# Scan: one 512 KB load of the cumulated rows for each chunk, x and y moved two tiles at a time every second chunk

## The reference, cut to what matters

```
x = silu(causal_conv(xn @ Wx.T))
b, c, dt = x @ Wb.T, x @ Wc.T, softplus(x @ Wdt.T + b_dt)    # 8 heads, state 64
state = exp(dt_t * a) * state + (dt_t * b_t) x_t             # 8192 steps, one after the other
y_t = c_t . state
out = groupnorm(y + d * x) * silu(z) @ Wout.T
```

## Time and profile before

| | us |
|---|---|
| median of 3 runs | 1229.94 |
| lowest and highest | 1228.64, 1230.48 |
| profiled execution, its own time | 1230.54 |
| its span in the profile | 1228.7 |
| scan, by the transposes L1553 | about 190 to 779 |

### The profile page before, as it was taken

One profiled execution on the slowest core, in us unless ns is written; L12 is line 12 of the kernel. 1 busy time (PEld: TensorE's weight loads), 2 busy tenths in 40 slices (PEclk: granted clock), 3 DMA queues, 4 the chain that ended last, 5 costly groups with the idle time before them and its releaser, 6 DMA issues.

```text
span 1228.7 us, 31470 instructions
## 1 busy us (share of the span) xinstructions
PE 1208.2 (98%) x12207; PEld 1012.2 (82%) x12207; DVE 949.7 (77%) x2028; ACT 611.8 (50%) x1279; POOL 796.4 (65%) x790
## 2 busy tenths in 40 slices
PE   8999999999999999999999999999999999999998
PEld 4666678888888888888888788898999889899998
DVE  7999977889876777777778667987777765776676
ACT  6999984434444443354344335543333332555454
POOL 4889955555555676776776648476666655576664
PEclk9999999999999999999999999999999999999999
DMA  9799756554455445555455456565544446799994
GB/s 298 261 337 356 288 214 170 149 157 146 157 157 160 154 146 170 161 150 164 149 148 168 126 171 212 190 156 91 109 91 90 97 87 125 251 320 322 336 332 166
DMA packets 140404, 231.40 MB, mean 188 GB/s; under 512 B 24416, under 2 KB 83040, under 8 KB 135648
## 3 DMA queue, kind: packets, MB, share of 16 engines
q1 hardware_dynamic: 127104, 212.10, 52.6%
q0 software_dynamic: 12288, 17.05, 8.1%
q10 hardware_dynamic: 864, 0.24, 0.1%
HBM read 147.81 MB, written 81.53 MB: 187 GB/s over the span
## 4 chain that ended last, share of the span: by engine, by line
PE 85%; DVE 5%; ACT 3%; DMA 3%; issue 2%; SPq 1%; POOL 1%; ACTq 0%; POOLq 0%; DVEq 0%
PE ps L1446 27%; PE ps L1808 11%; PE ps L2067 9%; PE ps L2301 7%; PE ps L2280 7%; PE ps L1527 4%; PE ps L1494 3%; PE ps L1553 3%; PE ps L1516 3%; PE ps L1538 2%; PE ps L1567 2%; PE ps L695 1%; DMA x_dram<-x 1%; PE ps L1787 1%; ACT tap L503 1%
## 5 line engine op out<-in xcount | busy, mean ns | idle before, releaser
L1408 ACT ACTIVATE decay<-tap,ncum 128x128 f32<-128x128 f32 x344 | 105.5, 389 | 191.7 <-POOL tap L1315 191.7
L1993 POOL DMA_INDIRECT ffn_dram<-ob,idx x64 | 110.5, 1727 | 81.8 <-DVE ob L1912 67.8
L2029 ACT ACTIVATE mid<-ps,b_up 128x512 f32<-128x512 f32 x96 | 66.1, 689 | 152.9 <-PE ps L1808 149.6
L1322 POOL TENSOR_TENSOR x_lo<-x,x_hi 128x512 fp32r<-128x512 f32 x56 | 76.9, 1372 | 100.4 <-ACT x_hi L1392 98.6
L1179 DVE TENSOR_TENSOR x_dt<-ps,dt 128x512 f32<-128x512 f32 x64 | 44.2, 691 | 126.4 <-PE ps L1553 126.3
L1446 PE MATMUL ps<-x_hi,w_hi_b 128*128 128x512 f32 x240 | 100.0, 416 | 2.0 <-issue 1.9
L1446 PE MATMUL ps<-x_hi,w_hi_c 128*128 128x512 f32 x240 | 99.3, 414 | 0.0
L2156 POOL TENSOR_SCALAR yc<-yc,gn_scale,gn_shift 128x512 f32<-128x512 f32 x56 | 76.3, 1374 | 33.1 <-DMA yc<-y_dram 33.1
L1446 PE MATMUL ps<-x_lo,w_hi_b 128*128 128x512 f32 x240 | 95.1, 396 | 0.0
L1408 ACT ACTIVATE decay<-cum_row,ncum 128x128 f32<-128x128 f32 x168 | 51.5, 391 | 86.8 <-POOL cum_row L1315 86.8
L1446 PE MATMUL ps<-x_lo,w_hi_c 128*128 128x512 f32 x240 | 94.2, 392 | 0.0
(11 more groups left out here) (321 smaller groups left out, 3996.9 us busy)
## 6 DMA issues: line engine op xcount, KB each, us to landing
tap<-cum_dram SPq DMA_DIRECT2D x86, 256.0 KB, 3.6
x_dram<-x SPq DMA_DIRECT2D x16, 1024.0 KB, 5.8
ecum_row<-ecum_dram SPq DMA_DIRECT2D x128, 128.0 KB, 3.7
yc<-y_dram SPq DMA_DIRECT2D x16, 1024.0 KB, 6.7
y_dram<-yb SPq DMA_DIRECT2D x60, 256.0 KB, 2.9
x<-x_dram SPq DMA_DIRECT2D x52, 256.0 KB, 3.9
cum_row<-cum_dram SPq DMA_DIRECT2D x42, 256.0 KB, 3.4
rows_dram<-xn SPq DMA_DIRECT2D x16, 512.0 KB, 3.3
```

The source lines that it names most:

```text
L1322: nc.gpsimd.tensor_tensor(low, raw, high, ALU.subtract).then_inc(x_lo_ready, 1)
L1408: n = nc.scalar.activation(decay[g % 2][:, h, :], cum_row[g % NR][:, row, :], ACT.Exp, bias=t.ncum[:, g, h:h + 1])
L1993: pool.indirect_dma_start(out=t.ffn_dram, out_offset=bass.IndirectOffsetOnAxis(ap=t.idx[:, e, h * HC + c:h * HC + c + 1], axis=0), in_=ob[ ...
```

## The change

Three transfers of the scan are regrouped, and SP's list is put in another order.

- The rows of a chunk come in one transfer of 512 KB, 4 KB for each partition, instead of two of 256 KB with 2 KB. It stands at the head of SP's list, right behind `x_turned`; it no longer waits for `b_turned` and `c_dec_ready`.
- y goes out two tiles at a time (512 KB), in chunks c = 0 and c = 2 of a block. It stands behind `b_turned` and the zeros. With c = 0 it waits for `y_ready` as before, with c = 2 for `c_dec_ready`.
- x comes in two tiles at a time (512 KB), in chunks c = 1 (tiles 2 and 3 of block b + 2) and c = 3 (tiles 0 and 1 of block b + 3), behind `c_ready` as before.
- The counts of the semaphores are fitted to the new numbers of transfers.

```diff
@@ SP's helpers @@
-        def load_cum(g, k):
+        def load_cum(g):
             until(sp, exp_ready, g - NR + 1)
-            rows = slice(k * H // 2, (k + 1) * H // 2)
-            sp.dma_start(cum_row[g % NR][:, rows, :], t.cum_dram[g, rows].partition_broadcast(P)).then_inc(
-                cum_loaded[g % NR], 16)
+            sp.dma_start(cum_row[g % NR][:, :, :], t.cum_dram[g].partition_broadcast(P)).then_inc(cum_loaded[g % NR], 16)
...
-            sp.dma_start(x2[b % NX][:, m, :], t.x2_dram[b, :, m, :]).then_inc(x2_loaded[b % NX], 16)
+            sp.dma_start(x2[b % NX][:, m:m + 2, :], t.x2_dram[b, :, m:m + 2, :]).then_inc(x2_loaded[b % NX], 16)
@@ SP's list for chunk g, after the wait for x_turned @@
-            if b:
-                if c == 0:
-                    sp.wait_ge(y_ready, CH * b)
-                until(sp, y_stored[(b - 1) % 2], y_stores(b - 1, c) - 16)
-                sp.dma_start(t.y_dram[b - 1, :, c, :], yb[(b - 1) % 2][:, c, :]).then_inc(y_stored[(b - 1) % 2], 16)
+            if g < LAST:
+                load_cum(g + NR - 1)
+                if g == LAST - 1:
+                    load_cum(LAST + 2)
...
-            if g < LAST:
-                if not last:
-                    sp.wait_ge(b_turned, updates(g) + 1)
-                load_cum(g + NR - 1, 0)
-                sp.wait_ge(c_dec_ready, g + 1)
-                load_cum(g + NR - 1, 1)
...
+            if not last:
+                sp.wait_ge(b_turned, updates(g) + 1)
             lanes = slice(c * P // CH, (c + 1) * P // CH)
             sp.dma_start(t.ffn_flat[b, lanes, :], zero[lanes, :]).then_inc(zero_stored, 16)
-            if b + NX < NB + (c < CH - 1):
-                sp.wait_ge(c_ready, g + 1)
+            if b and c % 2 == 0:
+                if c == 0:
+                    sp.wait_ge(y_ready, CH * b)
+                else:
+                    sp.wait_ge(c_dec_ready, g + 1)
+                until(sp, y_stored[(b - 1) % 2], y_stores(b - 1, c) - 16)
+                sp.dma_start(t.y_dram[b - 1, :, c:c + 2, :], yb[(b - 1) % 2][:, c:c + 2, :]).then_inc(
+                    y_stored[(b - 1) % 2], 16)
+            if c % 2 and b + NX < NB + (c < CH - 1):
                 if c == CH - 1:
+                    sp.wait_ge(c_ready, g + 1)
                     load_x2(b + NX, 0)
                 elif b:
-                    load_x2(b + NX - 1, c + 1)
+                    sp.wait_ge(c_ready, g + 1)
+                    load_x2(b + NX - 1, 2)
```

More of the change, by code:

```diff
@@ L971, in y_stores @@
     def y_stores(b, m):
-        return 16 * (MT * (b // 2) + m + 1)
+        return 16 * (2 * (b // 2) + m // 2 + 1)
     def x_loads(b, m):
-        return 16 * (MT * (b // NX - 1) + m + 1 + b % NX // 2) if b >= NX else 16
+        return 16 * (2 * (b // NX - 1) + m // 2 + 1 + b % NX // 2) if b >= NX else 16
     def listed(g):
@@ L1250, in _ @@
         for g in range(NR - 1):
-            for k in range(2):
-                load_cum(g, k)
+            load_cum(g)
         store_rows(1)
@@ L1266, in _ @@
             elif g == LAST:
-                for k in range(2):
-                    load_cum(NT - 1, k)
+                load_cum(NT - 1)
                 x.load_down(sp, 0)
-            if b:
-                if c == 0:
-                    sp.wait_ge(y_ready, CH * b)
-                until(sp, y_stored[(b - 1) % 2], y_stores(b - 1, c) - 16)
-                sp.dma_start(t.y_dram[b - 1, :, c, :], yb[(b - 1) % 2][:, c, :]).then_inc(y_stored[(b - 1) % 2], 16)
+            if g < LAST:
+                load_cum(g + NR - 1)
+                if g == LAST - 1:
+                    load_cum(LAST + 2)
             if g == 2:
@@ L1277, in _ @@
                              t.gates[:, :, :]).then_inc(t.gates_stored, 16)
-            if g < LAST:
-                if not last:
-                    sp.wait_ge(b_turned, updates(g) + 1)
-                load_cum(g + NR - 1, 0)
-                sp.wait_ge(c_dec_ready, g + 1)
-                load_cum(g + NR - 1, 1)
-                if g == LAST - 1:
-                    for k in range(2):
-                        load_cum(LAST + 2, k)
+            if not last:
+                sp.wait_ge(b_turned, updates(g) + 1)
             lanes = slice(c * P // CH, (c + 1) * P // CH)
             sp.dma_start(t.ffn_flat[b, lanes, :], zero[lanes, :]).then_inc(zero_stored, 16)
-            if b + NX < NB + (c < CH - 1):
-                sp.wait_ge(c_ready, g + 1)
+            if b and c % 2 == 0:
[7 more added lines that the diff above has]
+            if c % 2 and b + NX < NB + (c < CH - 1):
                 if c == CH - 1:
+                    sp.wait_ge(c_ready, g + 1)
                     load_x2(b + NX, 0)
                 elif b:
-                    load_x2(b + NX - 1, c + 1)
+                    sp.wait_ge(c_ready, g + 1)
+                    load_x2(b + NX - 1, 2)
             if g + 2 < NT:
@@ L1306, in causal @@
         def causal(g):
-            pool.wait_ge(cum_loaded[g % NR], 2 * loads(g, NR))
+            pool.wait_ge(cum_loaded[g % NR], loads(g, NR))
             even, odd = (cum_row[g % NR][:, k * H // 2:(k + 1) * H // 2, :] for k in range(2))
@@ L1978, in _ @@
             if e == 2:
-                sp.wait_ge(t.y_stored[1], 16 * (MT * (NB // 2 - 1) + 1))
+                sp.wait_ge(t.y_stored[1], 16 * (2 * (NB // 2 - 1) + 1))
                 sp.wait_ge(t.stat_done, MT * NB)
@@ L2332, in _ @@
         for q in range(2):
-            sp.wait_ge(t.y_stored[q], 16 * (MT * (NB // 2) if q == 0 else MT * (NB // 2 - 1) + 1))
+            sp.wait_ge(t.y_stored[q], 16 * (2 * (NB // 2) if q == 0 else 2 * (NB // 2 - 1) + 1))
         sp.wait_ge(x.turned, KT * (NU - 2))
```

## The result

The kernel with the change took 1222.09 us in the median (1221.62 to 1223.66, four runs), the kernel before, on the same chip, 1230.21 (1228.64 to 1233.21). The ratio is 0.9934, with a 95% interval of 0.9919 to 0.995. The profiled execution took 1222.01 us with a span of 1220.2, against 1230.54 and 1228.7: 8.5 us less. The prediction said 1224 in a range of 1220 to 1233.

What follows compares the result with a forecast made beforehand. PE, busy 98%, was taken to bound the kernel, losing time to program pages late behind data. Terms -2.62 - 0.9 - 3.7 + 1.1 = -6.1 us took the profiled 1230.54 to 1224.4, stated as a 1224 median, range 1220 to 1233.

Steps and rivals of the forecast that it cites:

- The mechanism: PE's six "issue" pauses in the scan, 6.3 us, are pages of its program arriving late behind data transfers.
- Odd-chunk pauses: Chunks with c = 1 or 3: pauses at 341.31, 602.69 and 700.51 us all gone, -2.62 us.
- The long pause and the clock: Pause at 688.77 us, out of g = 52: its 1.89 us and 1.8 us of clock gone, -3.7 us.
- Even-chunk pauses: Chunks with c = 0 or 2: pauses at 331.39 and 481.60 us, 1.79 us, half of it gone, -0.9.
- New pauses: Chunks with c = 1 or 3: the doubled x transfer ahead of the narrow part adds one pause, +1.1 us.
- Fewer issues, rows earlier: SP's queue has 120 fewer issues and POOL's waits for rows should go; each worth 0 in itself.
- The start: First load of rows as one 512 KB transfer: between -0.4 and +0.9 us, taken as 0.
- The cover: The c = 2 y store lands 0.9 us late for POOL; c_dec has 3.76 us to spare, so cost 0.
- the point of decision: Rival on POOL's chain: y stores landing later than 6.9 us slow PE, up to 21 us; chance 0.05.
- As late as before: Rival: program pages come as late, six pauses stay or as many others come, 1230 us; chance 0.26.
- more pauses: Rival: x's 512 KB just before the narrow part doubles the pauses, +6.3 us, 1236 us; chance 0.11.
- All pauses go: Rival: all scan pauses, the clock loss and 0.4 us at the start vanish, -8.5, 1221.4 us; chance 0.08.

Runs made afterwards that it cites:

- before_shift: The kernel before, with PE's 29 opening matmuls each cut into two of half the width, 58 more instructions ahead of the scan: 1227.07 us, ratio 0.9949.
- rows_one_mid: The kernel before, with a chunk's rows in one 512 KB transfer at their old mid-chunk place: 1227.55 us, ratio 0.9977.
- rows_one_head: The kernel before, with a chunk's rows in one 512 KB transfer at the head of SP's list, x and y tile by tile: 1222.56 us, ratio 0.9911.
- after_halves: The change, with the rows in two 256 KB transfers, both at the head of SP's list: 1224.1 us, ratio 0.994.
- pairs_only: The change, with the rows in halves and back behind b_turned and c_dec_ready, x and y still in pairs: 1246.22 us, ratio 1.0139.
- after_ecum_head: The change, with the load of ecum_row also moved to the head of the next chunk's list: 1226.36 us, ratio 0.9944.

## Why the prediction was right

**The mechanism.** Right, with a wrong measure in it. The pauses are the program's pages (before_shift, and the packets, which end 1.2 to 1.7 us before PE goes on), and the rows' place in SP's list sets their length (rows_one_mid against rows_one_head, which differ in nothing else). Wrong is the block of data counted by its bytes: a write of 512 KB is through sooner than a load of 512 KB and delays the page by 0.5 us instead of 1.7. One count was off too: four of the six pauses lie in L1494, as the earlier trace rows has it, not three; nothing rests on it.

**The terms.** The sum was -6.1 us, measured were -8.5.
- *Odd-chunk pauses*, -2.62, all gone: nearly so, -2.35. 341.31 and 602.69 are gone from the chain; of 700.51 0.27 is left.
- *The long pause and the clock*, -3.7: as said. The clock is 1.00 where it was 0.66.
- *Even-chunk pauses*, -0.9 of 1.79: -1.1, with 0.38 and 0.30 left.
- *New pauses*, +1.1: none came. This is the term that was mis-sized. I had put it in because x, now 512 KB, leaves just ahead of the narrow part. In chunk 43 of the kernel after x is issued at 597.75, within 0.1 us of the start of the page's packet, and the DMA share from 597.1 to 598.1 is 0.06: x's data come behind the page.
- These sum to -5.3 of pauses against -4.3 foreseen (2.62 + 0.9 + 1.89 - 1.1), and -1.8 of clock, as foreseen.
- *Not foreseen*: -1.5 in the last three chunks, where a pause of 0.94 us before (773.43) is in no list of mine, since I had stopped at 756 us; +0.9 at the casts of g = 58; -0.8 in the places named above.
- *Fewer issues, rows earlier*: 0 each, and nothing in the profile speaks against it.
- *The start*, 0: 0.4 us later here, inside my bounds, and not to be told. The first transposes of the fourteen profiles stand at 190.06 to 191.09 us in no order of the first load's size (190.21 in rows_one_head with 512 KB, 191.07 in after_halves with 256). The rows land in 4.1 us, the lower end of what I gave.

**The cover.** POOL's slack held: y's store landed in 2.8 us, 3.5 at worst, where the point of decision was 6.9. I had guessed 4, and a wait of POOL's of 1 us in every second chunk; there were seven waits, the longest 6.1. pairs_only shows the cover taken away: some 17 us more than the kernel before (0.0139 of 1230), whose rows stand as late, and some 25 more than the change (1.0139 - 0.9934).

**The rivals.** "As late as before" and "more pauses" rested on as many bytes ahead; the bytes were no measure. "All pauses go", 1221.4, was nearly what came, with 1.0 us left, and I gave it 0.08: too little, since I took y's 512 KB for as great a hindrance as the rows had been. That the time came within 0.7 us of it is luck in part: 1.4 of the 8.5 us lie in terms that are in no list of mine.

**What is left.** The 0.3 us at 480.41 of the kernel after look as if no data had been in the way, since from 478 to 480 us the queues carry

```profile
q1 hardware_dynamic: 12, 0.02, 3.6%
q8 instruction: 1, 0.02, 3.1%
```

But the packet is that of this pause; it starts near 478.4, 7.2 us into the chunk. Just ahead of it y's pair goes out: from 477.0 to 477.8 the data queue has

```profile
q1 hardware_dynamic: 81, 0.31, 95.3%
```

In rows_one_head, with y tile by tile, the same packet starts 6.7 us into the chunk and 0.03 us of the pause is left. So this 0.3 belongs to y in pairs.

**Open.** Why a page's packet waits at all for data on another queue, and what sets the 6.7 us at which it goes when nothing is in the way: the trace shows when a packet moves, not when it was asked for.

## What to carry to other kernels

When one engine is busy 98% and its remaining gaps are called "issue", put each beside the last packet of the queue of instruction transfers: here a late page showed by a packet that ended 1.2 to 1.7 us before the engine went on. Test the reading by adding a few dozen instructions ahead; pauses that move with them are pages of the program. Here the place of the loads around the densest stretch of instructions was worth 0.7% and their size nothing that shows; the gain came from moving the large load to where each instruction lasts long. Look at what the transfers put behind the load hold: the same pairs cost 0.1 to 0.2% behind early rows, less than the intervals can tell, and some 17 us behind late ones.

## What the runs showed that I had not expected

- A load of 512 KB issued in mid-chunk brings pauses of up to 1.65 us (rows_one_mid), a write of 512 KB at that place none over 0.4, since the write's data are through when the page goes.
- PE's clock fell behind a standstill of 1.89 us (granted 0.66 over 5 us), and didn't behind those of 1.65 and 1.45 us of rows_one_mid (granted 1.00 in the 5 us behind each). The length alone doesn't decide it: after_ecum_head stands still for 2.04 us at 767.90, and in the 5 us from 770 on 1.00 is granted:

```profile
770.00:775.00 5.00, 4.32 (x66) 1.00 0.51 138
```

- A shift of the program by 58 instructions was worth 0.5% by itself. Two kernels that differ in the number of PE's instructions can differ by as much for this reason alone.
- One cast of 32x16 took 1.80 us instead of 0.17 where POOL's 128x512 `c_dec` ran beside it, in ten profiles of ten in which the two met.
